# An attention stage: the loads at its start split over two queues, value and gate bias added by VectorE, output projection as three split products

## The reference

```python
x = x + 0.5 * ffn(layernorm(x))
x = x + attn(layernorm(x))        # the stage of this case, and the experts behind it
x = x + 0.5 * ffn(layernorm(x))

def attention(x, ...):            # 16 heads of 16, chunks of 64 tokens
    q = phi(apply_rope(heads(x @ Wq + bq)))      # phi(x) = elu(x) + 1
    k = phi(apply_rope(heads(x @ Wk + bk)))
    v = heads(x @ Wv + bv)
    g = heads(jax.nn.sigmoid(x @ Wg + bg))
    # per chunk:
    S = S + jnp.einsum('bhtd,bhte->bhde', kc, vc); Z = Z + kc.sum(axis=2)
    num = jnp.einsum('bhtd,bhde->bhte', qc, S)
    den = jnp.einsum('bhtd,bhd->bht', qc, Z)[..., None] + 1e-06
    out = gc * (num / den)
    return out @ Wo + bo
```

## Time and profile before

| what | us |
|---|---|
| runs before the change (3) | 2402.76, 2406.5, 2407.63, median 2406.5 |
| the profiled execution | 2401.99 |
| its span | 2400.2 |
| mean granted TensorE clock over the span | 0.961 of full |
| attention, from the issue of its first load to the first instruction behind it | 782.7 to 1063.6 |
| busy over the span: PE, DVE, ACT, POOL | 2251.5, 1650.8, 906.9, 871.1 |

### The profile page before, as it was taken

One profiled execution on the slowest core, in us unless ns is written; L12 is line 12 of the kernel. 1 busy time (PEld: TensorE's weight loads), 2 busy tenths in 40 slices (PEclk: granted clock), 3 DMA queues, 4 the chain that ended last, 5 costly groups with the idle time before them and its releaser, 6 DMA issues. The chain is left out here.

```text
span 2400.2 us, 37916 instructions
## 1 busy us (share of the span) xinstructions
PE 2251.5 (94%) x13564; PEld 1953.9 (81%) x13564; DVE 1650.8 (69%) x3575; ACT 906.9 (38%) x1704; POOL 871.1 (36%) x920
## 2 busy tenths in 40 slices
PE   6998999999999799966999999978998999999998
PEld 5887888888888577745889999966887888888887
DVE  5775777777776566656766666745775777777775
ACT  5222333333333566641323333325222333333332
POOL 4201233323332677732414444434201323333332
PEclk9998999999999799987989999988998999999999
DMA  5003354444443411112314444434013444445452
GB/s 179 27 27 120 109 137 130 120 127 132 132 112 69 148 34 36 34 54 74 82 37 85 85 84 85 81 67 145 27 36 118 117 132 128 132 113 141 124 133 45
DMA packets 154107, 228.04 MB, mean 95 GB/s; under 512 B 33344, under 2 KB 104512, under 8 KB 153920
## 3 DMA queue, kind: packets, MB, share of 16 engines
q1 hardware_dynamic: 102368, 157.16, 21.0%
q0 software_dynamic: 39936, 55.93, 13.6%
q10 hardware_dynamic: 11616, 12.53, 1.6%
HBM read 171.16 MB, written 54.39 MB: 94 GB/s over the span
## 5 line engine op out<-in xcount | busy, mean ns | idle before, releaser
L1182 ACT ACTIVATE me_act_f<-me_in,me_bias 128x512 f32<-128x512 f32 (+1 forms) x192 | 119.0, 620 | 300.5 <-PE me_in L142 300.5
L1182 ACT ACTIVATE f2e_silu<-f2e_in,f2e_bias 128x512 f32<-128x512 f32 (+1 forms) x136 | 90.2, 663 | 340.8 <-PE f2e_in L142 292.9
L1182 ACT ACTIVATE f1e_silu<-f1e_in,f1e_bias 128x512 f32<-128x512 f32 (+1 forms) x136 | 90.1, 663 | 340.8 <-PE f1e_in L142 292.9
L140 PE MATMUL f2e_in<-f2e_xt_hi,f2e_w_hi 128*128 128x512 f32 (+1 forms) x544 | 208.7, 384 | 3.8 <-DVE f2e_xt_lo L1250 2.3
L140 PE MATMUL f1e_in<-f1e_xt_hi,f1e_w_hi 128*128 128x512 f32 (+1 forms) x544 | 208.4, 383 | 4.0 <-DVE f1e_xt_lo L1250 2.3
L142 PE MATMUL f2e_in<-f2e_xt_hi,f2e_w_lo 128*128 128x512 f32 (+1 forms) x544 | 207.9, 382 | 0.0
L142 PE MATMUL f1e_in<-f1e_xt_hi,f1e_w_lo 128*128 128x512 f32 (+1 forms) x544 | 207.8, 382 | 0.0
L141 PE MATMUL f2e_in<-f2e_xt_lo,f2e_w_hi 128*128 128x512 f32 (+1 forms) x544 | 207.4, 381 | 0.0
L141 PE MATMUL f1e_in<-f1e_xt_lo,f1e_w_hi 128*128 128x512 f32 (+1 forms) x544 | 207.2, 381 | 0.0
L140 PE MATMUL me_down<-me_w_hi,me_act_hi 128*128 128x256 f32 x640 | 184.8, 289 | 0.0
L141 PE MATMUL me_down<-me_w_lo,me_act_hi 128*128 128x256 f32 x640 | 180.9, 283 | 0.0
(11 more groups left out here) (453 smaller groups left out, 6980.0 us busy)
## 6 DMA issues: line engine op xcount, KB each, us to landing
f_raw<-in_ffn_w SPq DMA_DIRECT2D x256, 384.0 KB, 3.8
m_raw<-in_moe_w SPq DMA_DIRECT2D x64, 256.0 KB, 2.9
f1s_x_all<-in_x SPq DMA_DIRECT2D x8, 512.0 KB, 9.1
after_ffn<-f1s_out SPq DMA_DIRECT2D x8, 512.0 KB, 2.9
after_moe<-ma_x_all SPq DMA_DIRECT2D x32, 128.0 KB, 1.7
m_h<-ma_h SPq DMA_DIRECT2D x32, 128.0 KB, 1.7
f2s_x_all<-after_moe SPq DMA_DIRECT2D x8, 512.0 KB, 9.0
out<-f2s_out SPq DMA_DIRECT2D x8, 512.0 KB, 2.9
```

Source lines behind the costliest of these rows:

```text
L140: pe.matmul(out, lh, rh, start=first, stop=False, skip_group_check=True)
L1182: act.activation(dst[:, st % 2, 0:n], ps_in[st % 2][0][:, 0:n], func, bias=bias[:, b, f:f + 1]).then_inc(silu_done, 1)
```

## The change

1. **Loads.** The nine constants move from ACT's queue to SP's: five of them (`ident`, `rope`, `bo`, `mask`, `wo`) behind the first pair of x loads, four (`norm2`, `router`, `cst`, `rb`) behind all x loads, with a semaphore of their own. The router is scaled in round 7 of DVE's list (`rotate(4)`). The zeros for `spare` are issued by ACT at the end of its program, directly before ACT waits for their landing.
2. **Head of the stage.** DVE does `stat(0)` before it splits the weights; ACT rounds the bias of q and k alone (512 columns), at the start of its round 2; DVE takes its low part behind `split_low(0)`.
3. **Bias of values and gates.** `project_vg` no longer starts with the product of `pick` and `bias_rows`. A new DVE step `add_vg_bias` (lag 4, between `stat` and `feature`) adds the bias while it reads `ps_vg`: gates to `g`, values to `v1`. ACT's `values` waits for `v1_done` and takes tanh of `g`; it keeps its place at the head of ACT's list.
4. **Output projection.** `ot` is split as `at` is: ACT rounds `ot_hi`, a new DVE step `split_o` (lag 6, before `add_out`) makes `ot_lo`. `project_o` is six fp32r matmuls of 256 columns in place of two fp32 ones; `wo` is split once.

```diff
         def project(r, ps, cols, done):
-                pe.matmul(ps[:], pick[:], bias_rows[:, cols], start=True, stop=False, skip_group_check=True)
...
             def project_o(r):
                 pe.wait_ge(ot_done, r + 1)
+                if r == 0:
+                    pe.wait_ge(wo_lo_done, 1)
                 for k in range(K):
-                    ins = pe.matmul(ps_o[:, 1, :], ot[:, r % 2, k, :], wo[:, k, :], start=(k == 0), stop=(k == K - 1))
+                    ins = product(pe, ps_o[:, 1, :], [x[:, r % 2, k * P:(k + 1) * P] for x in (ot_hi, ot_lo)],
+                                  [x[:, k, :] for x in (wo_hi, wo_lo)], k == 0, k == K - 1)
...
-            for dst, src in ((ident[:], consts[:, C_IDENT:C_IDENT + P]),
...
-                act.dma_start(dst, src).then_inc(const_in, 16)
-            act.wait_ge(set_up, 1)
-            act.dma_start(spare.rearrange("(t p) d -> p t d", p=P),
-                          zeros[:, 0:D].unsqueeze(1).to_broadcast([P, MOE_CAP // P, D])).then_inc(spare_out, 16)
...
             def values(r):
                 u = r % 2
-                act.wait_ge(vg_done, r + 1)
+                act.wait_ge(v1_done, r + 1)
                 if r >= KEPT:
                     act.wait_ge(o_done, r - KEPT + 1)
-                if r >= 2:
-                    act.wait_ge(s1_done, r - 1)
-                else:
-                    act.wait_ge(set_up, 1)
-                act.activation(tanh[:, r % KEPT], ps_vg[:, D:2 * D], ACT.Tanh, scale=0.5)
-                act.copy(v1[:, u, :, 0:P], ps_vg[:, 0:D].rearrange("p (k c) -> p k c", k=2)).then_inc(v1_done, 1)
+                act.activation(tanh[:, r % KEPT], g[:, u], ACT.Tanh, scale=0.5).then_inc(tanh_done, 1)
...
             rounds([(4, values), (11, keep_score), (5, copy_qt), (4, exp_rot), (3, copy_qk), (6, copy_ot), (10, copy_ht),
-                    (2, split_at), (1, norm), (7, sum_squares), (9, normalise_h)])
+                    (2, split_at), (1, norm), (7, sum_squares), (9, normalise_h)], after=(2, round_bias))
+            act.dma_start(spare.rearrange("(t p) d -> p t d", p=P),
+                          zeros[:, 0:D].unsqueeze(1).to_broadcast([P, MOE_CAP // P, D])).then_inc(spare_out, 16)
             act.wait_ge(spare_out, 16)
...
+            def add_vg_bias(r):
+                u = r % 2
+                dve.wait_ge(vg_done, r + 1)
+                if r >= 2:
+                    dve.wait_ge(s1_done, r - 1)
+                    dve.wait_ge(tanh_done, r - 1)
+                dve.tensor_tensor(g[:, u], ps_vg[:, D:2 * D], bias[:, 3 * D:4 * D], ALU.add)
+                dve.tensor_tensor(v1[:, u, :, 0:P], ps_vg[:, 0:D].rearrange("p (k c) -> p k c", k=2),
+                                  bias[:, 2 * D:3 * D].rearrange("p (k c) -> p k c", k=2), ALU.add).then_inc(v1_done, 1)
...
             def divide(r):
                 dve.wait_ge(num_done, r + 1)
+                dve.wait_ge(tanh_done, r + 1)
...
+            def split_o(r):
...
+                dve.wait_ge(ot_hi_done, r + 1)
+                dve.tensor_tensor(ot_lo[:, r % 2], ps_o[:, 0, :], as_f32(ot_hi[:, r % 2]), ALU.subtract).then_inc(ot_done, 1)
...
-            weights_low()
-            rounds([(6, divide), (5, state0), (0, stat), (4, feature), (3, rotate), (5, state1), (2, split_low),
-                    (6, add_out)], after_first=bias_low)
+            rounds([(6, divide), (5, state0), (0, stat), (4, add_vg_bias), (4, feature), (3, rotate), (5, state1), (2, split_low),
+                    (6, split_o), (6, add_out)], after=(1, weights_low))
```

More of the change, by code:

```diff
@@ L1439, in attention @@
             s.sb(n, [P, 2, 2 * D]) for n in ("qk", "rot_a", "rot_b", "rot", "er", "pos_part", "phi"))
-        tanh = s.sb("tanh", [P, KEPT, D])
+        tanh, g = s.sb("tanh", [P, KEPT, D]), s.sb("g", [P, 2, D])
         v1 = s.sb("v1", [P, 2, 2, HW])
@@ L1482, in loaded, with rounds @@
             return x_in_s[i][r % 2]
-        def rounds(steps, after_first=None):
+        def rounds(steps, after=None):
             for n in range(T + max(lag for lag, _ in steps)):
-                if n == 1 and after_first:
-                    after_first()
+                if after and n == after[0]:
+                    after[1]()
                 for lag, step in steps:
@@ L1495, in _, with load @@
             last.wait(sp)
-            for i, (q0, q1) in enumerate(LOADS):
+            def load(i):
+                q0, q1 = LOADS[i]
                 for u in range(2):
@@ L1499, in _ @@
                                  ).then_inc(x_in_s[i][u], 16)
+            load(0)
+            for dst, src in ((ident[:], consts[:, C_IDENT:C_IDENT + P]),
+                             (rope[:].rearrange("p q c j -> p q (c j)"), w["rope"]),
+                             (bo[:], w["bo"].to_broadcast([P, D])),
+                             (mask[:], consts[:, C_MASK:C_MASK + HW]), (wo[:], w["wo"])):
+                sp.dma_start(dst, src).then_inc(const_in, 16)
+            for i in range(1, len(LOADS)):
+                load(i)
+            for dst, src in ((norm2[:], w["norm2"]), (router_raw[:], w["router"]), (cst[:], consts),
+                             (rb[:], w["router_b"].to_broadcast([P, MOE_E]))):
+                sp.dma_start(dst, src).then_inc(late_in, 16)
             def store_total(r):
@@ L1617, in project_qk @@
                     pe.wait_ge(rot_a_done, r)
+                pe.matmul(ps_qk[:], pick[:], bias_rows[:], start=True, stop=False, skip_group_check=True)
                 project(r, ps_qk, QK, qk_done)
@@ L1699, in _, with round_bias @@
                 act.activation(w_hi[:, k], w_raw[:, k], ACT.Copy, scale=scale[:, k:k + 1]).then_inc(w_hi_done, 1)
-            act.wait_ge(bias_in, 16)
-            act.copy(bias_rows[:], bias[:]).then_inc(rows_rounded, 1)
+            def round_bias():
+                act.wait_ge(bias_in, 16)
+                act.copy(bias_rows[:], bias[:, QK]).then_inc(rows_rounded, 1)
             def norm(r):
@@ L1753, in copy_ot @@
                     act.wait_ge(wo_done, r - 1)
-                act.copy(ot[:, r % 2].rearrange("p k c -> p (k c)"), ps_o[:, 0, :]).then_inc(ot_done, 1)
+                act.copy(ot_hi[:, r % 2], ps_o[:, 0, :]).then_inc(ot_hi_done, 1)
+                if r == 0:
+                    act.wait_ge(const_in, 16 * N_CONST)
+                    act.copy(wo_hi[:], wo[:]).then_inc(wo_hi_done, 1)
             def sum_squares(r):
```

27 lines of the change are left out of this document (16 added, 11 removed).

## The result

The change makes the kernel slower: 2462.06 us median of four runs (2460.87 to 2464.07), against 2404.63 for the kernel before on the same chip (2402.35 to 2407.63). The ratio is 1.0246, 95% interval 1.0233 to 1.0259. The profiled execution has a span of 2459.2 us, 59.0 over that of before, with a mean clock of 0.952 for 0.961.

A forecast was written before the change was run, and what follows sets the result against it. PE's list bounded a middle round at 7.93 us; after the change a chain of waits would, at 9.15. Rounds +42, zeros +5, head -3.5 sum to +43.5, giving 2450 us; range 2436 to 2468, chance 0.85.

The forecast's parts named there:

- the forecast by itself: Attention stage: a chain of 9.15 us a round sets the pace, 2439 to 2461 us; chance 0.80.
- three upper bounds: Round without the overlaps taken off, +7; zeros 6.5 us where 5 was taken; head gaining nothing where -3.5 was taken.
- The chain: Attention rounds: waits from divide through additions, tanh, feature, split_o and project_o to the next divide make 9.15 us, against 7.93.
- PE's own list: Attention rounds: PE's work falls from 7.93 to 7.60 us, 0.23 by the bias product and 0.10 by project_o.
- The loop in the middle: 23 middle rounds of attention: each 9.15 us instead of 7.93, +28 us in all.
- 23 x 1.22: The middle's term: 23 rounds, each 1.22 us longer, +28 us.
- The clock falls: Rival: PE's idle gaps bring half clock, near 12 us a round; 2466 if a fifth fall, 2530 if all; chance 0.10.
- The early rounds: First five rounds of attention: the chain holds them too, 45.8 us against 36.6, +9.2.
- The fill: Before the first numerators: the same two steps delay two rounds by about 0.5 us each, +1.
- The last three rounds: End of attention: the chain fades, 8.2, 7.5 and 5.2 us, 20.9 against 16.7, +4.
- The zeros: End of the stage: the store for spare, now issued last by ACT, is uncovered, +5 us (3 to 6.5).
- The head: Start of the stage: ACT, freed of issuing DMAs, starts on weights earlier, -3.5 us; best 6.1, worst 1 lost.

The follow-up runs named there:

- experiment 1: The changed kernel with tanh (the step values) moved in ACT's list from first place to behind the exponential: 2405.35 us, ratio 1.0014.
- experiment 2: The changed kernel with add_vg_bias moved to first place in DVE's list, before divide: 2403.25 us, ratio 1.0003.
- experiment 3: The changed kernel with project_o as the plain fp32 product again, without split_o; late additions and tanh first stay: 2411.23 us, ratio 1.003.
- experiment 4: The changed kernel with the bias of values and gates on PE again and tanh reading PSUM; split projection stays: 2406.47 us, ratio 1.0012.
- experiment 5: The changed kernel with the zeros for spare issued in ACT's round 7 instead of at its program's end: 2453.6 us, ratio 1.0223.
- experiment 7: The changed kernel with nine extra, overwritten 256-column products on PE before each wait for ot_done: 2451.23 us, ratio 1.0212.
- experiment 6: The kernel before with only the new load order, the new head and the zeros at the end: 2403.96 us, ratio 1.0006.
- experiment 9: The kernel of experiment 8 with split_o back behind split_low in DVE's list: 2395.52 us, ratio 0.9973.
- experiment 10: The kernel of experiment 8 with ten extra, overwritten products per round on PE from round 27 on: 2395.96 us, ratio 0.9969.
- experiment 8: The changed kernel with add_vg_bias first in DVE's list, split_o ahead of state1, and the zeros issued early: 2392.64 us, ratio 0.9955.

## Why the prediction was right, and where it was short

The forecast was slower by 43.5 us, 2450; measured 57.4, 2462.06. That is inside the range of 2436 to 2468, but 1 us above the 2439 to 2461 that I gave the forecast by itself, so it lies in the part of the range that I had left for a falling clock. (My three upper bounds, +7, +1.5 and +3.5, add up to 2462, or to 2463 with the 1 us lost at the head, not to 2461.) The chain and the length of a round were right by their mechanism; that the errors of the other terms stayed within the range is in part luck. Point by point:

- **The chain** is right link by link. From the start of `divide`: tanh at 3.31 (said 3.30), `feature` 5.14 (5.14), `rotate` 5.75 (5.76), `state1` 6.35 (6.38), `ma_ot_lo` 7.03 (7.08), `project_o` 7.50 (7.55), numerators 8.39 (8.40), next `divide` 9.14 (9.15). Experiments 1 to 4 show it as the cause of the long rounds in the middle: break it at any one of the joints they tried, and 7.5 to 7.8 remain.
- **PE's own list** was said to be 7.60 and is 7.53 (experiment 2). The bias was 0.23 as said, the split projection saves 0.17, not 0.10. I took 0.70 from the first to the sixth product out of rows behind a wait, where the first product takes 0.23; in experiment 2, where PE doesn't wait, it is 0.58, and 0.21 from there to the numerators. Behind the wait of the changed kernel it is 0.69 and 0.20, so 0.89 in the chain for my 0.85.
- **The loop in the middle**, +28 said, +30.7 measured. The term that was mis-sized is "23 x 1.22": three rounds of the 23 were 10.63, 9.50 and 10.63. The two of 10.63 go with a fallen clock, 0.60 from 957 to 964 us and 0.69 from 1060 to 1071. There a product of 512 columns took a slot of 0.43 us, not 0.23. "The clock falls" came true in part beside the forecast, not in its place. One such dip cost 1.48 us, less than the 2.9 of my 12 us for a fallen round, because it covered a part of a round, and the wait for `ma_ot_lo` absorbed some: there was none in the long round. The 9.50 is not the clock's: in this round, the twelfth of the 23, DVE stands still for 0.30 us before the additions without a wait that the profile shows ("issue"). The twelfth round has the same stop, and is as much longer, in experiment 5 (9.52), in experiment 7 at full clock (9.50) and in experiment 1 (8.00 for 7.65). What the stop is stays open. The last of the 23 was shorter than the chain, 8.41.
- **The early rounds**, +9.2 said, +11.0 measured. The first two were 9.92 and 10.68, 2.3 us above 9.15 together, and most of it is a term that I had put at nothing: the low part of `wo` (0.60) and the scaling of the router (1.29), both on DVE's part of the chain. The clock, 0.68 in the second of the two rounds and full in the first, adds less: `ma_state` of DVE waited 0.40 for PE there. The next three were 9.16, 8.91 and 8.90: without the copy of scores in front of the exponential the chain is a little shorter, where I had said that it holds unchanged.
- **The fill** (from the first product to the first `divide`), +1 said, +3.5 measured, with a granted clock of 0.68 in it where it had been 0.85. The new loads are not the cause: in experiment 6 the fill takes 15.92 us. It takes 15.94 without the additions (experiment 4) and 16.07 with tanh behind the exponential (experiment 1), but 19.69 with the late additions and without `split_o` (experiment 3). So the late additions lengthen it when ACT has to wait for them at the head of its list. The clock goes with some 2 us of it: experiment 7 is the same program up to its first filler, and took 17.71 at a clock of 0.77. How much is the wait's and how much the clock's was not separated.
- **The last three rounds**, +4 said, +8.6 measured: 8.10, 8.65 and 8.55 for my 8.2, 7.5 and 5.2. I let the chain fade with its work. But from 1093 us to ACT's last copy PE ran at half clock (0.50): in the round from 1087.51, PE first waited 3.1 us for `ma_ot_lo`, still as part of the chain, and six products and the numerators then took 2.8 us where they take 1.6.
- **The end**: I had no term for the way from the last `divide` to ACT's last copy, and it costs +3.5, at a clock of 0.50 (0.96 before). It is 13.4 us in each of the seven kernels where the clock is 0.50 there (the changed one and experiments 1 to 5 and 9), and 10.4 in the two with fillers (experiments 7 and 10), where it is 0.94 and 0.96.
- **The zeros**: +5 said, +5.2 measured by the trace and 5.5 by the times (experiment 5). The Trainium skill (DMA: Bandwidth & Descriptors, "Anatomy of one DMA") gives for another kind of queue what makes an estimated 5.0 us; the trace agrees, with 5.2 from issue to landing.
- **The head**: -3.5 said, -3.6 measured to the first product. In experiment 6, where all four bias rows are still rounded, it was -2.1 (784.77 to 800.38).

Of the 15 us by which the stage is longer than forecast (58.9 for 43.5), two thirds are at its ends (fill +2.5, last rounds +4.6, way out +3.5), and in all of them the granted clock is below that of before. It is the size of three terms that failed, and two terms that were missing, the way out and the two steps that run once. For the clock two experiments are interventions. With PE kept busy in every round (experiment 7), middle, last rounds and way out together are 7.0 us shorter, while the five early rounds are 3.2 longer; with PE kept busy at the end of another kernel (experiment 10), the way out is shorter. What makes the clock fall at the end is argued from the windows, and not shown.

The Trainium skill (TensorE: Matmul & The Clock Gate, "HAM oscillation") says that a wait which returns with every tile of a matmul kernel can bring the half clock back each time; the waits of its example, for a DMA, are longer than those here. The trace agrees in part: with a gap of some 1.35 us in nearly every round, eleven rounds from 857 to 957 us kept a clock of 1.00, and then one fell to 0.60.

## What to carry to other kernels

When a step moves from the engine that is full to one with idle time, look at the place it gets in that engine's queue, not at the idle time: late in DVE's list the two additions closed a loop that cost 58 us (by the ratios of the changed kernel and of experiment 2), and ahead of a wait that was there anyway they cost nothing in the middle of the stage. Draw the loop once around (which engine waits for which, from `divide` to `divide`) with start-to-start distances from the trace; a loop can be closed by two edits that are each harmless alone in the steady rounds, so test them apart and together, and look at the first and last rounds by themselves: there each was not harmless. A step that runs only once costs its full time when it stands on the chain. Then move whatever others wait for ahead of what they don't, as the kernel of experiment 8 does, and see what an unhidden transfer at a barrier costs.

## What was not expected of the hardware

- A granted clock that falls after rounds which all look alike: PE was busy some 83% of the time (33.24 of 40 us), with the same gap in each round, and the clock was 1.00 from 857 to 957 us and 0.60 right behind. In experiment 5, with the same loop, the rounds at a fallen clock were others (those that end at 885.69 and 988.19).
- More products made the program faster (experiment 7, by 8.2 us by the ratios and some 4 by the trace), and in experiment 10 fifty of them gained nothing (3.4 us slower by the ratios, with intervals that overlap). The clock has to be weighed against what the filler itself costs.
- One subtraction's place decided whether the last two rounds took 9.2 or 14.5 us (experiments 8 and 9), although DVE was busy for only 6.33 of the 14 us in the slower one. That half clock and waits feed each other where a stage runs out of work would explain it; what lets the clock fall there was not tried.
